# Attention maxima turned on TensorE, sent from ScalarE, with contiguous query tiles

## The reference

```
xn = layernorm(x)
h = (xn - mean) * rsqrt(var + eps) * ln_scale + ln_bias
c_q, c_kv = h @ w_down_q.T, h @ w_down_kv.T            # 256 -> 128
q, k, v = c_q @ w_up_q.T, c_kv @ w_up_k.T, c_kv @ w_up_v.T   # 16 heads of 64
q, k = rope(q), rope(k)
attn = softmax(q @ k.T / 8)
s = (attn @ v) @ w_out.T + xn
g = silu(moe(xn) + xn)       # 8 experts, top 2, capacity 2561
out = x + s * g
```

## Time and profile before

| what | us |
|---|---|
| median of 3 runs (3739.72 to 3741.53) | 3740.14 |
| the profiled execution, its own time | 3740.14 |
| its span, first to last instruction | 3738.6 |
| TensorE matmul busy | 3675.4 (98%) |
| TensorE weight load busy | 2475.6 (66%) |
| VectorE busy | 3202.6 (86%) |
| ScalarE busy | 2745.2 (73%) |
| GpSimd busy | 1198.5 (32%) |
| DMA engines, mean rate over the span | 194 GB/s |

### The profile page before, as it was taken

How to read it: one execution, slowest core, us unless ns; L and a number is a source line. 1 busy time by engine, 2 the same in 40 slices (tenths; PEclk the granted TensorE clock), 3 DMA queues, 4 the chain that set the end, 5 groups by cost and what they waited for, 6 DMA issues and landing times. The chain is left out here.

```text
span 3738.6 us, 75778 instructions
## 1 busy us (share of the span) xinstructions
PE 3675.4 (98%) x23720; PEld 2475.6 (66%) x23720; DVE 3202.6 (86%) x4340; ACT 2745.2 (73%) x3888; POOL 1198.5 (32%) x1178
## 2 busy tenths in 40 slices
PE   7989999999999999999999999999999999999999
PEld 5755555555555555555555555555599999999998
DVE  8868888888888888898888888888777777777799
ACT  5767778777777778787877777787766666666665
POOL 2202222222222222222222222223266666666500
PEclk9999999999999999999999999999999999999999
DMA  7975666666676666666666666665566666666797
GB/s 263 355 253 138 169 164 170 163 160 173 158 180 152 181 155 177 155 172 166 166 166 160 176 152 180 155 179 141 145 227 222 221 217 216 216 216 222 232 368 272
DMA packets 413250, 724.73 MB, mean 194 GB/s; under 512 B 141117, under 2 KB 288702, under 8 KB 377088
## 3 DMA queue, kind: packets, MB, share of 16 engines
q0 software_dynamic: 83504, 340.66, 35.5%
q1 hardware_dynamic: 329680, 383.25, 31.4%
HBM read 453.60 MB, written 138.81 MB: 158 GB/s over the span
## 5 line engine op out<-in xcount | busy, mean ns | idle before, releaser
L1173 ACT ACTIVATE at_ex<-at_st 128x1024 f32<-128x1024 f32 x1024 | 1049.0, 1025 | 126.9 <-PE at_st L1311 121.0
L1324 PE MATMUL at_pv<-at_ex,at_v 128*64 128x512 f32 x4096 | 991.8, 605 | 0.0
L1031 DVE TENSOR_REDUCE at_mx<-at_fr 128x1 fp32r<-128x512 f32 x1024 | 704.7, 688 | 276.0 <-PE at_fr L1334 246.5
L1197 ACT ACTIVATE at_fr<-at_fr 128x512 f32<-128x512 f32 x1024 | 605.3, 591 | 351.3 <-PE at_fr L1334 336.5
L1331 PEld LDWEIGHTS at_fr<-at_kdif,at_qh 64*128 64x128 f32 x1024 | 312.9, 306 | 421.8 <-issue 359.3
L1324 PEld LDWEIGHTS at_pv<-at_ex,at_v 128*64 128x64 f32 x4096 | 248.7, 136 | 486.2 <-issue 486.2
L1044 DVE TENSOR_TENSOR at_sum<-at_sum,at_ex 128x1024 f32<-128x1024 f32 x448 | 544.8, 1216 | 3.5 <-ACT at_ex L1173 3.2
L1334 PE MATMUL at_fr<-at_kfar,at_qh 64*128 64x512 f32 x1024 | 531.5, 519 | 5.0 <-DVE at_mx L1031 4.5
L1331 PE MATMUL at_fr<-at_kdif,at_qh 64*128 64x512 f32 x1024 | 528.6, 516 | 3.9 <-DVEq L674 2.5
L1828 PE MATMUL ex_o<-ex_w,ex_hT 128*128 128x256 f32 x3408 | 426.0, 285 | 0.9 <-DVE ex_out L1693 0.9
L1812 PE MATMUL ex_h<-ex_xT,ex_w 128*128 128x256 f32 x3408 | 421.2, 283 | 1.6 <-DVE ex_w L1646 1.6
(11 more groups left out here) (205 smaller groups left out, 5995.0 us busy)
## 6 DMA issues: line engine op xcount, KB each, us to landing
at_cq<-scr_c SPq DMA_DIRECT2D x62, 1024.0 KB, 6.1
at_ck<-scr_c SPq DMA_DIRECT2D x62, 1024.0 KB, 5.0
at_sum<-at_sum POOLq DMA_DIRECT2D x95, 512.0 KB, 6.1
scr_v<-pj_v SPq DMA_DIRECT2D x64, 512.0 KB, 6.9
at_v<-scr_v SPq DMA_DIRECT2D x64, 512.0 KB, 6.8
mid_rec<-scr_rec SPq DMA_DIRECT2D x256, 128.0 KB, 3.9
scr_o<-mid_oT SPq DMA_DIRECT2D x64, 512.0 KB, 3.0
at_rotq<-at_swpq POOLq DMA_DIRECT2D x126, 256.0 KB, 4.8
```

Source lines behind the costliest of these rows:

```text
L1031: e.reduce_max(mx[k // QB][:, h * QB + k % QB:h * QB + k % QB + 1], fr[h][:, :], AX.X).then_inc(s_tr[h], 1)
L1173: e.activation(ex[k][:, :, :], st[u % 2][:, :, :], ACT.Exp, scale=SCALE).then_inc(s_exp, 1)
L1197: e.activation(fr[h][:, :], fr[h][:, :], ACT.Relu).then_inc(s_pos[h], 1)
L1324: mm = e.matmul(pv[n][rows[h], :], v[i.u][:, kt, rows[h]], ex[kt][:, h, :], start=(kt == 0), stop=(kt == KT - 1))
```

## The change

The maxima now stay in the order of the queries. `mx[n]` (128 partitions, 8 columns, now plain fp32) is transposed on TensorE to 8 partitions of 128 columns in the PSUM tile `pv[n]` (`turn_maxima`), ScalarE copies it with a factor of -1 to a new tile `mneg[n]` (`negate`), and ScalarE's own DMA queue sends its two groups of four rows to the row of `top` (`max_rows`). `one_row` is +1 now. Since the row comes out in plain order, `query_tile` is a contiguous slice of 128 queries. On VectorE both additions of a round stand behind the second maximum, and `normalise` and `recip` move.

```diff
-        mx = [sb(f"mx{n}", [P, 2 * QB], F32R) for n in range(NH2)]
+        mx = [sb(f"mx{n}", [P, 2 * QB]) for n in range(NH2)]
+        mneg = [sb(f"mneg{n}", [2 * QB, P], F32R) for n in range(NH2)]
...
-            def max_rows(j, n):
-
-                for h in range(2):
-                    e.wait_ge(s_tr[h], j.n(NSLOT_Q, QB * (n + 1)))
-                    r = rows[h].start
-                    e.dma_start(top[j.u][r:r + 1, bank[n]].bitcast(F32).rearrange("o (p t) -> o p t", p=P),
-                                mx[n][:, h * QB:(h + 1) * QB].bitcast(F32)).then_inc(s_mrow[n], 16)
...
@@ sync body @@
-                max_rows(i, 1)
                 if ahead >= 3:
                     load(i.next(3), K)
                 if prev:
                     spread(prev, (0, 1))
-                if ahead:
-                    max_rows(i.next(1), 0)
-                if prev:
...
@@ vector @@
-                    wait(e, s_mrow[k // QB], j.n(32))
+                    wait(e, s_tf, j.n(2, k // QB - 1))
...
-                    last = e.memset(one_row[r:r + 1, :].bitcast(F32), -1.0)
+                    last = e.memset(one_row[r:r + 1, :].bitcast(F32), 1.0)
...
+                    if g == 2 and older:
+                        normalise(prev.next(-1), 0)
...
+                    if g == 6 and older:
+                        normalise(prev.next(-1), 1)
...
-                    early, late = additions(i, prev, g)
-                    for added in early:
-                        add_keys(*added)
                     if g < 2 or more:
                         maximum(*slot_of(i, g), 0, s_y)
-                    for added in late:
-                        add_keys(*added)
+                    if g:
+                        add_two(i, 2 * g - 2)
+                    elif prev:
+                        add_two(prev, UNITS - 2)
...
-                    if g == 4 and older:
-                        normalise(prev.next(-1), 0)
...
-                    if g == 7 and prev:
+                    if g == 6 and prev:
                         recip(prev)
-                    if g == 7 and older:
-                        normalise(prev.next(-1), 1)
...
@@ scalar @@
+            def negate(j, n):
+                e.wait_ge(s_tf, j.n(2, n + 1))
+                wait(e, s_mrow[n], j.n(32, 0))
+                e.activation(mneg[n][:, :], pv[n][0:2 * QB, 0:P], ACT.Copy, scale=-1.0).then_inc(s_neg, 1)
+
+            def max_rows(j, n):
+                e.wait_ge(s_neg, j.n(2, n + 1))
+                for h in range(2):
+                    r = rows[h].start
+                    e.dma_start(top[j.u][r:r + 1, bank[n]].bitcast(F32).rearrange("o (t q) -> o t q", q=P),
+                                mneg[n][h * QB:(h + 1) * QB, :].bitcast(F32)).then_inc(s_mrow[n], 16)
...
                     exps(i, 2 * g)
+                    if g == 3 and more:
+                        max_rows(i, 1)
+                    if g == 7 and more:
+                        max_rows(one, 0)
...
+                    if g == 2:
+                        negate(i, 1)
+                        if not more:
+                            max_rows(i, 1)
...
+                    if g == 6 and more:
+                        negate(one, 0)
...
@@ tensor @@
             def query_tile(j, k, h):
-                return hi[Q][j.u][rows[h], bank[k // QB]].rearrange("d (p t) -> d t p", t=QB)[:, k % QB, :]
+                return hi[Q][j.u][rows[h], k * P:(k + 1) * P]
...
+            def turn_maxima(j, n):
+                for h in range(2):
+                    e.wait_ge(s_tr[h], j.n(NSLOT_Q, QB * (n + 1)))
+                e.transpose(pv[n][0:2 * QB, 0:P], mx[n][:, :], keep["ident"][:, :]).then_inc(s_tf, 1)
...
+                    if g == 2:
+                        if ahead >= 2:
+                            e.wait_ge(s_raw[K], two.n(2, 1))
+                        else:
+                            e.wait_ge(s_osb, i.n(2, 0))
+                        turn_maxima(i, 1)
                     if g == 3 and ahead >= 2:
-                        e.wait_ge(s_raw[K], two.n(2, 1))
+                        e.wait_ge(s_neg, i.n(2, 2))
                         project(two, K, 1, pv[1])
...
+                    if g == 6 and ahead:
+                        if ahead >= 3:
+                            e.wait_ge(s_raw[Q], three.n(2, 1))
+                        else:
+                            e.wait_ge(s_osb, i.n(2, 1))
+                        turn_maxima(one, 0)
                     if g == 7 and ahead >= 3:
-                        e.wait_ge(s_raw[Q], three.n(2, 1))
+                        e.wait_ge(s_neg, one.n(2, 1))
                         project(three, Q, 1, pv[0])
```

More of the change, by code:

```diff
@@ L770, in attend_parts @@
         s_tr = [sem(f"tr{h}") for h in range(2)]
+        s_tf, s_neg = sem("tf"), sem("neg")
         s_mrow = [sem(f"mrow{n}") for n in range(NH2)]
@@ L886, in prologue @@
                     e.sem_inc(s_ld[x][0], 16)
-                e.wait_ge(s_init, 2)
-                max_rows(At(0, 0), 0)
             def body(i, prev, ahead):
@@ L1044, in add_keys, with add_two @@
                 e.tensor_tensor(out=acc, in0=ex[k - 1][:, :, :] if first else acc, in1=ex[k][:, :, :], op=ALU.add).then_inc(s_sum, 1)
[L1046 to L1050, removed]
+            def add_two(i, u):
+                n, k = u // KT, u % KT
+                for m in (k, k + 1):
+                    if m % (KT // 2):
+                        add_keys(i, n, m)
             def recip(i, halves=slice(0, 2), k=0):
@@ L1147, in tail @@
             def tail(i):
-                for n, k in ((1, KT - 2), (1, KT - 1)):
-                    add_keys(i, n, k)
+                add_two(i, UNITS - 2)
                 for n in range(NH2):
@@ L1235, in prologue @@
                         pj_value(2 * k + 2)
+                    if k == 4:
+                        negate(first, 0)
                     if k == 5:
@@ L1242, in prologue @@
                         pj_value(2 * k + 3)
+                    if k == 4:
+                        e.wait_ge(s_init, 2)
+                        max_rows(first, 0)
                 proj_copy(third, Q, 1, pv[1])
@@ L1420, in prologue @@
                         next(choice)
+                    if k == 4:
+                        e.wait_ge(s_raw[K], 3)
+                        turn_maxima(first, 0)
                     step_y(first, k)
@@ L1439, in bank_free @@
                         e.wait_ge(s_raw[Q], two.n(2, 2))
-                    elif n == 0 and prev:
-                        e.wait_ge(s_osb, i.n(2, -1))
                     elif n == 0:
-                        e.wait_ge(s_raw[K], 4)
+                        e.wait_ge(s_neg, i.n(2, 1))
                     elif prev:
@@ L1463, in side @@
                         else:
-                            e.wait_ge(s_osb, i.n(2, 0))
+                            e.wait_ge(s_neg, i.n(2, 2))
                         denominators(prev)
```

## The result

| | us |
|---|---|
| changed kernel, median of 4 runs (3763.82 to 3766.67) | 3764.25 |
| before, beside it, median of 4 runs (3737.14 to 3741.53) | 3739.93 |
| ratio | 1.0067 (1.005 to 1.0085) |
| profiled execution, span | 3763.3 |
| predicted | 3685 (3650 to 3745) |

The kernel became 0.67% slower, some 25 us, where I had forecast 55 us off. The prediction was wrong in its direction.

What follows compares the result with a forecast made beforehand. TensorE was taken to bound the attention stretch (busy 699 of 700 us). Shorter weight loads -102, transposes +28 and VectorE's order +19 gave -55 us: 3740.1 to 3685 us, range 3650 to 3745.

Steps and rivals of the forecast that it cites:

- VectorE reordered: VectorE's order within a pair of heads: maxima come late into rounds 1 and 7, costing 19 us, ends 0 and 38.
- Rival B: VectorE in the attention rounds becomes the bound, four rounds of a pair losing 0.2 us: 51 us, 3717 us; chance 0.12.
- Step y's gain: Second max matmuls of each round, behind score matmuls: shorter weight load saves 0.08 us each, 512 times, 41 us.
- Step x's gain: Max matmuls opening each round, behind value matmuls: shorter weight load saves 0.12 us each, 512 times, 61 us.
- rival C: Max matmuls' weight loads: the query tile's stride isn't why they are slow, only transposes' 28 us remain, 3768 us; chance 0.04.
- Transposes: Two per pair on TensorE, in rounds 2 and 6: 128 at 0.22 us cost 28 us, ends 19 and 58.
- ScalarE's issues: Sending maxima rows from ScalarE, rounds 3 and 7: 0.5 us each, hidden in idle time, cost 0; 64 us if slow.
- the landing: Arrival of the maxima row before scores of units 8 and 0: 2.2 us against 3.25 us of slack, wait 0.
- Rival A: The maxima row lands late and TensorE waits: at 4.0 us of landing it costs 96 us, 3781 us; chance 0.12.

Runs made afterwards that it cites:

- old-order kernel: Changed kernel with VectorE's old order: one addition between a round's two maxima, normalisations in rounds 4 and 7, reciprocal in 7; 3693.37 us, ratio 0.9886.

## Why the prediction was wrong, step by step

**The step that failed: "VectorE reordered", "64 x 0.3 = 19 us; ends 0 and 38".** It was sized at 19 us and took 68. The mechanism was seen, at the right place for two of its three rounds, and its size was missed. From the table of step y distances, new against old order in the changed kernel: 38.40 - 37.26 = 1.14 us of a pair, 73 us; the measured ratios say 68. Four parts of my working were off. (1) Two additions in a row take 2.39 us, not 2 x 1.13: the second adds to the sum of the first and waits for its semaphore, so it starts 1.25 us after it (the row of 2.47 us for two, less the 1.22 of one). (2) I let the maximum end 0.60 after its start, which is when the next instruction starts; TensorE sees it after 0.68. (3) From there to step y it takes another 0.15 us. These three make the loop 4.28 us where my figures give 3.91 (1020.10 to 1024.01). TensorE's own work in that round is 3.92, where they give 3.84, since step y kept its 0.32 us; so step y is 0.36 us late where I took 0.1 to 0.2. (4) Round 3 was left out, and behind each late step y the load lies bare, 0.11 us. Rival B, which I gave 0.12, named the engine, but by total load ("33.8 us of work in 37.1"); that was the wrong measure. VectorE idles for 0.79 us in the round in which it makes TensorE wait. What decides is a loop between two engines within one round.

A second term failed too, the gain of step y below. Between the forecast change of -55 us and the measured +25 lie 80 us: this term has 49 of them (68 for 19) and step y 41, while steps x (66 for 61) and transposes (23 for 28) came out 5 us better each. By these sums the first error alone would have left 3734 us and the second alone 3726, both inside the range; it took the two together.

**Step y's gain, "512 x 0.08 = 41 us".** It was 0: a step y on time has 0.32 us before and 0.33 with the contiguous tile alone. The earlier trace rows had shown it: the record of step y starts 0.24 us after the one ahead and lasts 0.40, both as an ordinary score matmul. The load stuck out on paper only. The long slot, 0.32 us, is still there with a short load. It lies between this record and the next one, where another kind of matmul follows; what makes it long, no run separates.

**Step x's gain, "512 x 0.12 = 61 us".** Right: 64 us by the slots and 66 on the chip for that edit alone. The stride was the cause of the slow load, since the tile's edit alone takes it from 306 to 184 ns; rival C falls. By the column-count rule of the Trainium skill ("TensorE: Matmul & The Clock Gate", section "LDWEIGHTS (loading the stationary operand)") the edit would have brought nothing: the trace disagrees, 306 against 184 ns for the same 128 columns.

**Transposes, "128 x 0.22 = 28 us".** Right: 0.20 us each (1018.62 to 1018.82 in the changed kernel), 26 us. Contiguous alone against the old-order kernel, which adds transposes and the new way of the row, is 0.62%, 23 us. In the changed kernel itself they are hidden, since they stand in the loops that lead to rounds 3 and 7, where TensorE has to wait anyway: 4.33 and 4.44 us, as in the kernel before with the new order (4.33 and 4.45), which has no transposes.

**ScalarE's issues and the landing, "0" each.** Right in the changed kernel. An issue took 581 ns in the median, at most 1196, and ran beside the exponential:

```profile
1022.00 1.03 ACT L1160 ACTIVATE at_ex<-at_st 128x1024 f32<-128x1024 f32 x1 [0.19 <-PE at_st L1325]
1022.03 1.20 ACTq L1205 DMA_DIRECT2D at_top<-at_mneg  x2
1023.28 0.58 ACT L1184 ACTIVATE at_fr<-at_fr 128x512 f32<-128x512 f32 x1 [0.25 <-PE at_fr L1345]
```

The two DMAs start 0.03 us into the exponential and are out 0.05 us before the next Relu. Rival A, the landing, did not happen; the profile has no landing times for this queue, but TensorE's waits have no such row. In kernels with shorter rounds it is late now and then: 3 times in the old-order kernel (1.1 us) and 14 times with the additions alone put back (5.9 us), so a wait of 0 holds for the changed kernel, and no wider.

Together, per pair, going from before over the old-order kernel to the changed one: steps x -1.00, transposes +0.40, late steps y +1.14, and -0.09 left over, of which 0.04 is in round 1 (a slot of 0.45 before, 0.41 in the old-order kernel): +0.45 us, the 38.40 - 37.95 of the table; 64 pairs make 29 us, and 25 were measured.

## What to carry to other kernels

Where two engines hand work back and forth, add up the loop (from one handing over to the same one in the next round, with each hand-over's own delay) for every round, and compare it with the bound engine's own time in that round; the share of busy time says nothing about it. A queue in program order wants its independent work in the gap before a wait, not behind the instruction that the wait releases. And before a long slot is put down to a load, look at whether the record itself starts late or lasts longer than its neighbours'.

## What the runs showed of the hardware that was not expected

A weight load of 306 ns cost nothing behind score matmuls that follow each other every 0.23 us: step y has a slot of 0.32 us with it (before) and 0.33 us with one of 184 ns (contiguous tile alone). Behind a wait the load counts: a late step y has a slot of 0.43 us with a 184 ns load (changed) and 0.55 us with a 306 ns load (changed, strided tile). So a late operand costs TensorE more than its lateness, here 0.11 and 0.23 us each time.
